# Causal mask of a self-attention moved from a TensorE product to VectorE, row-maximum subtraction moved from VectorE to GpSimd

## The reference

```python
x = x + _L0_attn_ref(_layernorm(x, axis=-1), wq, wk, wv, wo)
...
scores = jnp.einsum('bhse,bhte->bhst', q, k) / scale
causal_mask = jnp.triu(jnp.ones((s, s), dtype=bool), k=1)
scores = jnp.where(causal_mask, jnp.asarray(NEG, scores.dtype), scores)
weights = jax.nn.softmax(scores, axis=-1)
heads = jnp.einsum('bhst,bhte->bhse', weights, v)
concat = heads.transpose(0, 2, 1, 3).reshape(b, s, N_HEADS * D_HEAD)
return concat @ wo.T
```

## Time and profile before

| | us |
|---|---|
| median of 3 runs (707.05 to 709.99) | 707.97 |
| the profiled execution, its own time | 707.11 |
| its span, first to last instruction | 705.3 |
| PE busy / DVE busy / ACT busy / POOL busy | 607.5 / 465.1 / 385.5 / 169.5 |

### The profile page before, as it was taken

One profiled execution on the slowest core, in us unless ns is written; L12 is line 12 of the kernel. 1 busy time (PEld: TensorE's weight loads), 2 busy tenths in 40 slices (PEclk: granted clock), 3 DMA queues, 4 the chain that ended last, 5 costly groups with the idle time before them and its releaser, 6 DMA issues. The chain is left out here.

```text
span 705.3 us, 18395 instructions
## 1 busy us (share of the span) xinstructions
PE 607.5 (86%) x6678; PEld 516.0 (73%) x6678; DVE 465.1 (66%) x981; ACT 385.5 (55%) x1009; POOL 169.5 (24%) x160
## 2 busy tenths in 40 slices
PE   3389688898989898998498999999999999769697
PEld 2377577777777787876387888889897988634397
DVE  3157376767777677677569975666657474647797
ACT  3157377776768676778344142433324252347895
POOL 4341515151423233240002031212203020241000
PEclk9779899999999999999699999999999999979899
DMA  7549554656565646351030000000000000000002
GB/s 238 134 120 318 122 141 115 155 122 149 134 149 132 151 99 160 91 118 40 17 104 2 2 2 1 0 0 0 0 0 0 1 2 2 1 9 0 1 31 91
DMA packets 33865, 52.08 MB, mean 74 GB/s; under 512 B 5377, under 2 KB 13697, under 8 KB 33825
## 3 DMA queue, kind: packets, MB, share of 16 engines
q1 hardware_dynamic: 29280, 42.75, 23.8%
q10 hardware_dynamic: 4352, 8.39, 4.1%
q0 software_dynamic: 192, 0.39, 0.2%
HBM read 17.96 MB, written 2.10 MB: 28 GB/s over the span
## 5 line engine op out<-in xcount | busy, mean ns | idle before, releaser
L548 ACT ACTIVATE Pr<-pS,nmax 128x256 f32<-128x256 f32 x256 | 119.2, 476 | 61.2 <-DVE nmax L644 60.2
L644 DVE TENSOR_REDUCE nmax<-pS 128x2 f32<-128x512 f32 x128 | 87.8, 687 | 74.1 <-PE pS L405 73.3
L326 POOL TENSOR_TENSOR Qst<-Qraw,rows_of 96x1024 fp32r<-96x1024 f32 x32 | 59.9, 1891 | 93.0 <-DMA Qraw<-QSh 90.1
L415 PE MATMUL pT<-ident,Pr 128*128 128x128 f32 x512 | 77.4, 273 | 0.2 <-ACT Pr L548 0.2
L860 POOL TENSOR_TENSOR a_Pr<-a_Pr,a_rinv 128x512 f32<-128x512 f32 x32 | 32.8, 1046 | 185.8 <-DVE a_rinv L1146 185.8
L405 PE MATMUL pS<-Kst,Qst 96*128 96x256 f32 x256 | 60.1, 317 | 15.0 <-POOL Qst L326 10.3
L1026 ACT ACTIVATE a_Pr<-a_Pr 128x512 f32<-128x512 f32 x32 | 20.2, 631 | 75.9 <-DVE a_Pr L1138 75.9
L415 PEld LDWEIGHTS pT<-ident,Pr 128*128 128x128 f32 x512 | 59.6, 141 | 0.4 <-ACT Pr L548 0.4
L405 PEld LDWEIGHTS pS<-Kst,Qst 96*128 96x128 f32 x256 | 40.3, 194 | 24.9 <-issue 14.3
L555 ACT ACTIVATE PT<-pT 128x512 f32<-128x512 f32 x64 | 38.2, 598 | 28.3 <-PE pT L415 26.7
L548 ACT ACTIVATION_READ_ACCUMULATOR Pr<-pS,nmax 128x1 f32 x256 | 52.5, 205 | 0.0
(11 more groups left out here) (258 smaller groups left out, 1852.1 us busy)
## 6 DMA issues: line engine op xcount, KB each, us to landing
Kst<-KSh SPq DMA_DIRECT2D x128, 128.0 KB, 2.5
CT<-ctxT ACTq DMA_DIRECT2D x16, 512.0 KB, 4.9
Kst<-KSl SPq DMA_DIRECT2D x64, 128.0 KB, 2.5
Qraw<-QSh SPq DMA_DIRECT2D x60, 64.0 KB, 2.0
X<-x SPq DMA_DIRECT2D x4, 512.0 KB, 8.7
out<-X SPq DMA_DIRECT2D x8, 256.0 KB, 2.1
Qraw<-QSl SPq DMA_DIRECT2D x30, 64.0 KB, 2.0
raw<-awq SPq DMA_DIRECT2D x1, 1024.0 KB, 6.7
```

Source lines behind the costliest of these rows:

```text
L326: last = pool.tensor_tensor(Qst[r][:, :, :, :, h2, :].rearrange("p j g a q -> p (j g a) q"), Qraw[:, :, r].rearrange("p j g a q -> p j (g ...
L415: last = pe.transpose(pT[s % 2][:, t, k, :], Pr[s % 2][:, t, P * k:P * k + P], ident[:, :])
L548: act.activation(Pr[c % 2][:, t, :], pS[c % 2][:, t, :], ACT.Exp, bias=nmax[c % 2][:, t:t + 1], accum_out=rsum[par][:, c // 4, 2 * (c % 4) ...
L644: dve.tensor_reduce(nmax[s % 2][:, :], pS[s % 2][:, :, :], AX.X, ALU.max, negate=True).then_inc(maxed, 1)
```

## The change

TensorE no longer multiplies the mask into PSUM; each score product starts and ends its own accumulation. VectorE adds `causal` to the scores while it moves them to `Pr`, and then takes the row maxima from `Pr` in SBUF. The subtraction of the maxima becomes a pass of GpSimd over `Pr`, ahead of ScalarE's exponential; GpSimd's order is now shift 0, shift 1, divide 0, divide 1, shift 2, shift 3, divide 2, divide 3. `rmax` has four buffers instead of one. A `sem_inc` by `apart` stands on TensorE between the waits and the score products.

```diff
--- before.py
+++ after.py
@@ -772,7 +772,7 @@
         QT = sb("QT", [P, HP, 2 * P], F32)
         KT = sb("KT", [P, HP, 2 * P], F32)
         V = sb("V", [P, 2, HE], F32)
-        rmax = sb("rmax", [P, 8], F32)
+        rmax = [sb(f"rmax{s}", [P, 8], F32) for s in range(4)]
         Pr = [sb(f"Pr{t}", [P, HP, 2, SQ], F32) for t in range(2)]
         rsum = [sb(f"rsum{s}", [P, 8], F32) for s in range(4)]
         rinv = [sb(f"rinv{s}", [P, 8], F32) for s in range(4)]
@@ -791,6 +791,7 @@
         ln_st, ln_mv, ln_ve, ln_rs, ln_xn = sem("ln_st"), sem("ln_mv"), sem("ln_ve"), sem("ln_rs"), sem("ln_xn")
         proj, xt_hi, xt_lo = sem("proj"), sem("xt_hi"), sem("xt_lo")
         by_act, by_dve = sem("by_act"), sem("by_dve")
+        masked = sem("masked")
         scored, maxed, shifted, exped, summed, inverted, weighted = (
             sem("scored"), sem("maxed"), sem("shifted"), sem("exped"), sem("summed"), sem("inverted"), sem("weighted"))
         turned, pt_done, pv_done, o_hi, o_lo, x_done = (
@@ -860,12 +861,21 @@
                 pool.tensor_tensor(rows, rows, rinv[s][:, :].unsqueeze(2).to_broadcast([P, 8, SQ]), ALU.mult
                                    ).then_inc(weighted, 1)
 
+            def shift(i, s):
+                pool.wait_ge(maxed, 4 * i + s + 1)
+                rows = Pr[s // 2][:, :, s % 2, :]
+                pool.tensor_tensor(rows, rows, rmax[s][:, :].unsqueeze(2).to_broadcast([P, 8, SQ]), ALU.subtract
+                                   ).then_inc(shifted, 1)
+
             rstd_of(0)
             rstd_of(1)
 
             def body(i, last):
-                for s in range(4):
-                    divide(i, s)
+                for t in range(2):
+                    shift(i, 2 * t)
+                    shift(i, 2 * t + 1)
+                    divide(i, 2 * t)
+                    divide(i, 2 * t + 1)
                 if two_ahead(i):
                     rstd_of(i + 2)
                 if not (isinstance(i, int) and i == 0):
@@ -919,16 +929,14 @@
                     pe.wait_ge(by_dve, len(BY_DVE) * i + 4)
                 after(pe, o_lo, 2 * (4 * i + 2 * t - 2))
                 out = [pS[2 * t + b][:, :].rearrange("p (j k) -> p j k", k=SQ) for b in range(2)]
-                for b in range(2):
-                    pe.matmul(pS[2 * t + b][:, :], identb[:, :], causal[:, :, :], start=True, stop=False,
-                              skip_group_check=True)
+                apart(pe, waited)
                 for j in range(HP):
                     for b in range(2):
                         tok = slice(P * t + SQ * b, P * t + SQ * b + SQ)
                         for h2 in range(2):
                             rows, side = slice(E * h2, E * h2 + E), (h2 + b) % 2
                             last = pe.matmul(out[b][SQ * side:SQ * side + SQ, j, :], QT[rows, j, tok],
-                                             KT[rows, j, tok], start=False, stop=True, skip_group_check=True)
+                                             KT[rows, j, tok], start=True, stop=True)
                 last.then_inc(scored, 2)
 
             def turn(i, s):
@@ -1127,16 +1135,14 @@
                 reused(dve, i, kind, part)
                 dve.tensor_copy(target(kind, part), pJ[bank][:, :]).then_inc(by_dve, 1)
 
-            def shift(i, s):
-
+            def mask(i, s):
                 n = 4 * i + s
+                rows = Pr[s // 2][:, :, s % 2, :]
                 dve.wait_ge(scored, n + 1)
-                after(dve, shifted, n)
-                scores = pS[s][:, :].rearrange("p (j k) -> p j k", k=SQ)
-                dve.tensor_reduce(rmax[:, :], scores, AX.X, ALU.max).then_inc(maxed, 1)
-                dve.wait_ge(maxed, n + 1)
-                dve.tensor_tensor(Pr[s // 2][:, :, s % 2, :], scores,
-                                  rmax[:, :].unsqueeze(2).to_broadcast([P, 8, SQ]), ALU.subtract).then_inc(shifted, 1)
+                dve.tensor_tensor(rows, pS[s][:, :].rearrange("p (j k) -> p j k", k=SQ), causal[:, :, :], ALU.add
+                                  ).then_inc(masked, 1)
+                dve.wait_ge(masked, n + 1)
+                dve.tensor_reduce(rmax[s][:, :], rows, AX.X, ALU.max).then_inc(maxed, 1)
 
             def sums(i, s):
                 dve.wait_ge(exped, 4 * i + s + 1)
@@ -1226,12 +1232,12 @@
                             copy(r, kind, part, k % 2, i)
 
                 first = isinstance(i, int) and i == 0
-                shift(i, 0)
-                shift(i, 1)
+                mask(i, 0)
+                mask(i, 1)
                 sums(i, 0)
                 sums(i, 1)
-                shift(i, 2)
-                shift(i, 3)
+                mask(i, 2)
+                mask(i, 3)
                 fills("V", 3)
                 fills("X", 0)
                 fills("X", 1)
```

## The result

The changed kernel takes 724.95 us (median of 4 runs, 722.67 to 725.92) against 708.98 us (4 runs, 707.05 to 711.06). The ratio is 1.0219, with a 95% interval from 1.0194 to 1.0243: 2.2% slower, where 727 us and 2.7% were forecast. The profiled span is 723.3 us, 18.0 more than before.

A forecast was written before the change was run, and what follows sets the result against it. TensorE sets the pace, and the chain from scores through VectorE to X1's bank has no slack. Span 705.3 + chain 10.5 + clock 9.0 + 1.8 around the span gives 726.6, for the median 727 us; range 715 to 734.

The forecast's parts named there:

- What bounds: Self-attention: TensorE sets the pace, but the chain from scores through VectorE to X1's bank has no slack and starts Q0.
- TensorE's saving: Mask products ahead of the scores: 0.44 us per pair saved, only the one ahead of score 0 being gain.
- The chain: Score 0 to Q0: mask 2 waits behind sums 1, Q0 starts 1.75 us later; net 1.31 us per quad, 10.5 in all.
- The clock: Idle ahead of X0 grows to 2.4 us per quad; the granted clock falls in 6 of 8 quads, 9.0 us in all.
- The sum: Whole kernel: span 705.3 plus 10.5 and 9.0, with 1.8 around the span 726.6; median forecast 727 us, 2.7% slower.
- A clock that holds: Rival, 17%: self-attention's chain grows but with no more than one or two clock falls; 718.5 us, up to 721.
- Dearer GpSimd passes: Rival, 8%: GpSimd's passes take 0.3 us more beside VectorE, 4.8 us on top; 732 us, 736 with all falls.
- The faster case: Rival, 4%: the chain is hidden and TensorE keeps its 7.0 us, 701 us; mask 2 would have to start at 5.2.

The follow-up runs named there:

- e1_no_mask: The kernel before with its mask products left out, each score product starting afresh behind `apart`: 703.83 us, ratio 0.993.
- e4_filled: The changed kernel with nine unused 512-column products on TensorE in the idle stretch ahead of X0 (last quad: turn 0): 717.9 us, ratio 1.0137.
- e5_dve_shift: The changed kernel with the subtraction of the maxima on VectorE instead of GpSimd: 737.72 us, ratio 1.0409.
- e10_dve_filled: e5_dve_shift with the nine filler products of e4_filled on TensorE: 725.69 us, ratio 1.0238.
- e7_order: The changed kernel with masks 2 and 3 ahead of sums 1 on VectorE, shifts 2 and 3 ahead of divide 1 on GpSimd: 710.17 us, ratio 1.0022.
- b1_three_masks: e6_scores with VectorE's mask 3 behind sums 1, GpSimd's shift 3 behind divide 1, ScalarE's high halves of X ahead of exponential 3: 702.89 us, ratio 0.9931.
- e6_scores: The changed kernel with score 1 right behind score 0, VectorE's four masks ahead of its sums, GpSimd's four shifts ahead of its divisions: 708.13 us, ratio 0.9988.
- e8_scores_q0: e6_scores with Q0 ahead of turns 0 and 1 on TensorE and its copy ahead of theirs on ScalarE: 717.65 us, ratio 1.0122.

## Why the prediction was right, step by step

**What bounds.** Right: the chain, not TensorE's order, started X1 and Q0 before. e1_no_mask shows it from the other side: about half of what was taken off TensorE was no gain.

**TensorE's saving.** 0.44 us per pair was taken, and only the one ahead of score 0 counted. e1_no_mask measured 0.45 at that place and 0.50 per quad. Score products that start afresh, with `apart`, take 472.25 - 471.16 = 1.09 us, as said.

**The chain.** Forecast 10.5 us in all. In e4_filled, where the clock is whole, score 0 to score 0 is 1.01 us longer in a steady quad (forecast 1.31) and the eight quads together some 9.5 us longer, because the first two and the last lost 1.5, 1.4 and 1.6. The difference in the steady quads is small steps: the maxima start 0.72 behind the mask's start and not 0.79, and the low halves follow each other at 0.34, so Q0 starts at 12.31 and not 12.6 with a whole clock. That the changed kernel's fourth quad has it at 12.60 is luck: the missing 0.3 is the low clock over X and the turns. The GpSimd pass was 1.04 for 1.03, the hop to ScalarE 0.04 for 0.03, V2's copy ended at 10.28 for 10.47. By the Trainium skill ("GPSIMD Engine Reference", Performance versus the Vector engine) the pass would have been an estimated 1.36 us; the trace doesn't agree at this size. The advice of the Trainium skill (the same reference, section Engine selection) to keep elementwise work on VectorE didn't hold here either: e5_dve_shift and e10_dve_filled were slower, because VectorE is the engine in the chain and GpSimd the idle one.

**The clock.** Six falls were forecast and six came in the profiled execution. The count is in part luck: no row gave it, and the last of the six lasted twice as long as the others. Their size was the step that was off: 1.5 us each, 9.0 in all, taken from one pair of quads of the cross-attention. In a steady quad a fall costs 34.03 - 33.04 = 0.99, and 1.8 us in the last quad, together 6.8 us by the trace and about 6 by the runs. The 1.5 was measured where TensorE had work throughout the low stretch. Here part of it lies over X and the turns, ahead of Q0, where TensorE would have waited 0.37 us for VectorE anyway; that is most of the difference. The rest is within what the cross-attention itself shows: there an earlier fall, in the quad from 164.76 to 202.72, cost 37.96 - 36.63 = 1.3 us.

**The sum.** The span grew by 18.0 us where 19.5 were forecast: 9.5 from the chain and 6.8 from the clock in the self-attention; the remaining 1.7 lies ahead of it and behind it, in stages that the change doesn't touch. So the total is nearer to the forecast than its terms: the chain came out 1.0 below and the clock 2.2 below, and 1.7 that nobody forecast made up for half of it.

**The rivals.** A clock that holds gave 718.5 in the prediction; e4_filled made that case and measured 717.9. Dearer GpSimd passes did not occur: 1,043 ns for the subtractions, 1,045 for the divisions. The faster case named mask 2 as the place that decides, and e7_order and b1_three_masks, which start it earlier, bear that out. What the prediction did not see is that this needs no faster pass, only another order.

## What to carry to other kernels

When work moves to an idle engine, follow the chain through every engine's queue: here a pass of 1 us cost 1.9 us per quad and another 1.0 through the clock, because the next tile's work was queued behind an instruction that waits for it and so the pass stood in the chain twice. Price the idle that results twice, as time and as clock, and check with filler products which of the two it is. The wait that a profile names at the stalled engine need not be the cost: removing it moved the stall to the next instruction, while another order of the same work made a loss of 2.2% a gain of 0.7%.

## What the runs showed of the hardware that was not expected

What follows on the clock is read from one profiled execution of each kernel; as e6_scores shows, others of the same kernel can differ. The same idle time did not always bring the clock down: the changed kernel idled 2.33 and 2.43 us in its first two quads at 1.00 and 2.27 us in the third with a fall. Falls then came in every quad, 34.1 us apart (447.8, 481.9, 516.1, 550.2, 584.3), in quads of 34.03 us, at nearly the same place of each. Less idle in two pieces can be enough: e8_scores_q0, with 0.69 and 1.02 us and only short transposes between, lost the clock in four of seven quads, while e7_order with 0.96 and 0.19 us did not in those quads, and neither did e6_scores with 0.70 and 0.41 in its profiled execution. What decides between these cases is open.

The maxima took 686 ns from SBUF, against 691 from PSUM before, and the addition with the BF16 mask 640 to 692 ns, no more than the subtraction with FP32 maxima.
